# Layer statistics placed elsewhere on VectorE, norms turned into rows before they are stored, and the rounded transposed context written by a converting DMA

## The chip, the cores and the metric

One core of one Trainium2 chip runs the program. A core has five engines that run their own instruction lists and meet only at semaphores: TensorE (PE, matmuls; its weight loads are listed as PEld), VectorE (DVE), ScalarE (ACT), GpSimd (POOL) and SyncE (SP, here only a queue that issues DMAs). The metric is the time of one execution on the device in microseconds (us).

## The reference

```python
# x (16,128,1024), ctx (16,128,1024); q and k channels are the 128 rows, n = 1024 columns
qh = Wq @ layernorm(x);  kh = Wk @ ctx;  vh = Wv @ ctx        # 8 heads of 64
qh = softmax(qh, over the 64 of a head) * 64**-0.5
kh = softmax(kh, over n)
context = kh @ vh.T                                            # per head, 64 x 64
out = Wo @ (context.T @ qh) + bo
out = out / max(sqrt(sum(out*out, over channels)), 1e-12) * g * sqrt(128)
x = x + tanh(g_xattn) * out
# then a routed feed-forward part
y = layernorm(x);  scores = y @ Wr.T;  top 16 of 64, softmax -> G
x = x + tanh(g_ffn) * 2.0 * ((y @ A) * G) @ B                  # 64 experts of rank 16
```

## The kernel before

The 16 batches are tiles of 128 partitions x 1024 values (512 KB). The kernel has two stages: attention over all batches, then the feed-forward part over all batches. Every large product is done in three passes: each operand is split into a rounded half (`_hi`, type fp32r) and the remainder (`_lo = value - _hi`), and `three_pass` (L52 to L54) multiplies hi*hi, lo*hi and hi*lo into the same PSUM bank. ACT or a copy makes the `_hi` part, DVE or POOL the `_lo` part.

**The attention stage.** Each engine runs `body(b, head, tail, ahead)`: the head of batch b beside the tail of batch b-1, with a few steps for b+1 ahead. Bodies 0, 1, 15 and 16 are written out and bodies 2 to 14 are a loop. Nothing reorders instructions: each engine runs its list as the code has it, and a step that waits holds everything behind it on that engine. The steps that matter here, by the names in the code:

- DVE `stats(b+1)` (L720, L723), with the Newton steps for 1/sqrt(variance) in `inv_std` (L67, L58, L71, and three times L73, L75) and `nbias` (L728): the layer norm of the next batch. It stands after `lo_k(b, 0)` and before `sum_q(b, 0)` (L764, L767) and `lo_q(b-1, 2)` (L773, writes `qT_lo`).
- ACT `norm_x(b+1)` (L477) waits for `nbias`; ACT `hi_c(b)` (L498) rounds the transposed context `ctxT_in` into `ctxT_hi` (`cT[0]`).
- POOL, in order: `halve` of the last q pair (L370, `qhalf`), `lo_xn`, two `normalise` (L377, in place on `qe`), `halve(b,0)`, `mt_lo` (L417), `normalise(b,0)`, `lo_ctx(b+1)` twice (L349), `halve(b,1)`, `lo_c(b)` (L354, makes `ctxT_lo`), `normalise(b,1)`, `lo_xn(b+1,0)` (L361), `halve(b,2)`.
- PE `tr_k`, `tr_q` (L1075, L1084) transpose into one PSUM pair `psT`. Each waits until DVE has read what stood there before: `tr_k(b,1)` waits for `lo_q(b-1,2)`. Then `shift_q` (L1065) waits for `max_q` (L759), and `mm_k(b+1,0)` needs `ctx_lo` of the next batch.

**The norms.** `square_norms` (L1128) sums squares with matmuls against a column of ones, one column of 128 norms for each 128 columns of a batch, into `psX[:, 1, :]`; `keep_norms` (L734) copies them to `ss`, and `root_norms` (L745 to L749) makes `rn = 1/sqrt(ss)` on DVE, once for batches 0 to 12 (104 columns) at the start of body 15 and once for batches 13 to 15 (24 columns) after body 16. SP `store_norms` writes `rn` to DRAM (`rn_scratch`) as single words. `load_attention` then reads `u_scratch` (the unnormalised output) and a broadcast row of `rn_scratch`, after the wait for the store.

**Between the stages.** At the end of POOL's body 15 stands `residual(0,0,0)` (L389, L393): u times rn, plus x, for batch 0. Behind it on POOL stands `halve(15,3)`. DVE's body 16 runs `sum_q(15,2)`, `sum_q(15,3)`, `stats2(0,0)` (L812 to L819), then ACT `normalise(0,0)` (L577) and PE `tr_y(0,0)` (L1141) start the feed-forward stage; PE's `fold(15)` and `output(15)` stand behind `tr_y(0,0)`. PE's first `up` matmuls need `aT_lo` from `lo_weight` (L803). The second stage is a chain of matmuls with a period of about 25.5 us a batch.

## Time and profile before

| | us |
|---|---|
| median of 3 runs (1084.74 to 1086.72) | 1085.11 |
| the profiled execution, whole | 1085.12 |
| its span in the profile | 1083.1 |
| PE, DVE, ACT, POOL busy | 991.4, 701.7, 490.1, 470.8 |
| mean granted share of TensorE's clock | 0.976 |

The span runs from the first to the last recorded instruction. Busy time is not the bound by itself: an engine that waits in each body, and is waited for, sets the time. So the profile is read by the waits of PE and by the chain that ended last.

### The profile page before, as it was taken

Reading aid. Unit: us, or ns where it says so; the run is one execution under the profiler, and the core shown is the slowest. Engines: PE = TensorE matmul, PEld = TensorE weight load, DVE = VectorE, ACT = ScalarE, POOL = GpSimd, SP = SyncE. Lnnn points to the kernel's source line nnn. Section 1 sums busy time; section 2 is a strip of 40 time slices with the busy share of each in tenths; the row PEclk is TensorE's granted clock in tenths of the full one; section 3 lists DMA queues with packets and bytes.
Section 4 is the critical chain, followed back from the end, with each engine's and each line's share of the span. In section 5 each row is a group of like instructions: output and inputs, shape, how many; then the busy total and the mean of one; then the engine's idle time right before and its main releaser. Section 6 shows DMA issues by size and latency. Waiting matters only on the chain.

```text
span 1083.1 us, 15822 instructions
## 1 busy us (share of the span) xinstructions
PE 991.4 (92%) x5200; PEld 821.6 (76%) x5200; DVE 701.7 (65%) x1349; ACT 490.1 (45%) x791; POOL 470.8 (43%) x301
## 2 busy tenths in 40 slices
PE   4899999999999999999999673899999999999997
PEld 3677877787787778778778562788888888888886
DVE  5687677768777876876778368555555555555321
ACT  4675677567566756766675462121111221111110
POOL 2755665475556546555645464322222233333000
PEclk9999999999999999999999986899999999999999
DMA  3115121122012112201209942222222222222000
GB/s 136 59 58 205 59 77 36 42 77 70 27 58 77 39 39 77 77 20 58 77 19 21 156 168 66 78 87 104 82 78 77 78 77 77 77 77 77 20 19 39
DMA packets 38470, 77.15 MB, mean 71 GB/s; under 512 B 19376, under 2 KB 19376, under 8 KB 38448
## 3 DMA queue, kind: packets, MB, share of 16 engines
q1 hardware_dynamic: 37296, 75.83, 23.5%
q10 hardware_dynamic: 1152, 1.05, 0.3%
q8 instruction: 10, 0.16, 0.1%
q14 instruction: 12, 0.10, 0.0%
HBM read 60.03 MB, written 16.84 MB: 71 GB/s over the span
## 4 chain that ended last, share of the span: by engine, by line
PE 69%; DVE 19%; issue 5%; DMA 4%; ACT 1%; POOL 1%; DVEq 0%; SPq 0%; ACTq 0%; POOLq 0%
PE ps L52 18%; PE ps L54 18%; PE ps L53 18%; PE ps L1084 4%; DMA rn_scratch<-rn 3%; DVE qT_lo L773 3%; PE ps L1152 3%; PE ps L1075 3%; PE ps L1128 2%; PE ps L1065 2%; DVE ekT_lo L780 2%; DVE bn L720 2%; DVE qmax L759 2%; PE ps L1173 2%; DVE kmax L754 2%
## 5 line engine op out<-in xcount | busy, mean ns | idle before, releaser
L377 POOL TENSOR_TENSOR qe<-qe,qrec 128x1024 f32<-128x1024 f32 x64 | 121.2, 1903 | 134.5 <-DVE qrec L767 134.5
L400 POOL TENSOR_TENSOR yT_lo<-yf,yT_hi 128x512 fp32r<-128x512 f32 x32 | 41.8, 1327 | 269.0 <-ACT yT_hi L600 269.0
L370 POOL TENSOR_TENSOR qhalf<-qe 128x512 f32<-128x512 f32 x64 | 82.3, 1287 | 89.5 <-ACT qe L524 89.5
L52 PE MATMUL ps<-aT_hi,yT_hi 128*128 128x512 f32 x256 | 102.2, 399 | 5.9 <-DVE aT_lo L803 5.9
L773 DVE TENSOR_TENSOR qT_lo<-ps,qT_hi 128x512 fp32r<-128x512 f32 x128 | 81.5, 679 | 32.8 <-ACT qT_hi L531 32.3
L52 PE MATMUL ps<-bT_hi,hT_hi 128*128 128x512 f32 x256 | 101.6, 397 | 0.0
L54 PE MATMUL ps<-aT_lo,yT_hi 128*128 128x512 f32 x256 | 100.3, 392 | 0.0
L53 PE MATMUL ps<-aT_hi,yT_lo 128*128 128x512 f32 x256 | 100.3, 392 | 0.0
L588 ACT ACTIVATE yf<-ps 128x512 f32<-128x512 f32 x32 | 17.5, 594 | 183.0 <-PE ps L1141 182.9
L53 PE MATMUL ps<-bT_hi,hT_lo 128*128 128x512 f32 x256 | 100.1, 391 | 0.0
L54 PE MATMUL ps<-bT_lo,hT_hi 128*128 128x512 f32 x256 | 99.9, 390 | 0.0
L1075 PE MATMUL ps<-ident,ek 128*128 128x128 f32 x512 | 70.4, 278 | 30.2 <-DVE qT_lo L773 30.2
L1075 PEld LDWEIGHTS ps<-ident,ek 128*128 128x128 f32 x512 | 58.9, 141 | 45.4 <-DVE qT_lo L773 33.5
L524 ACT ACTIVATE qe<-ps 128x1024 f32<-128x1024 f32 x64 | 65.7, 1026 | 46.7 <-PE ps L1065 46.7
L780 DVE TENSOR_TENSOR ekT_lo<-ps,ekT_hi 128x512 fp32r<-128x512 f32 x128 | 81.9, 682 | 5.5 <-ACT ekT_hi L538 5.5
L759 DVE TENSOR_REDUCE qmax<-ps 128x16 fp32r<-128x1024 f32 x64 | 77.9, 1216 | 9.2 <-PE ps L54 9.2
L754 DVE TENSOR_REDUCE kmax<-ps 128x1 f32<-128x1024 f32 x64 | 78.0, 1218 | 5.2 <-PE ps L54 4.5
L538 ACT ACTIVATE ekT_hi<-ps 128x512 fp32r<-128x512 f32 x128 | 70.8, 601 | 22.9 <-PE ps L1075 22.8
L516 ACT ACTIVATE ek<-ps,kmax 128x1024 f32<-128x1024 f32 x64 | 71.8, 1122 | 15.6 <-DVE kmax L754 15.6
L604 ACT ACTIVATE hT_hi<-ps 128x512 fp32r<-128x512 f32 x32 | 19.1, 598 | 127.7 <-PE ps L1173 127.6
L531 ACT ACTIVATE qT_hi<-ps 128x512 fp32r<-128x512 f32 x128 | 70.7, 599 | 11.6 <-PE ps L1084 10.5
L872 DVE TENSOR_TENSOR hg<-ps,gate 128x512 f32<-128x512 f32 x32 | 22.1, 691 | 82.6 <-PE ps L54 82.5
(134 smaller groups left out, 2523.5 us busy)
## 6 DMA issues: line engine op xcount, KB each, us to landing
ctx_in<-in_ctx SPq DMA_DIRECT2D x16, 512.0 KB, 3.7
x_in<-in_x SPq DMA_DIRECT2D x16, 512.0 KB, 3.2
ctxT_in<-in_ctxT SPq DMA_DIRECT2D x16, 512.0 KB, 3.3
u_scratch<-osb SPq DMA_DIRECT2D x16, 512.0 KB, 2.8
x<-in_x SPq DMA_DIRECT2D x16, 512.0 KB, 4.0
u_in<-u_scratch SPq DMA_DIRECT2D x16, 512.0 KB, 3.4
rn_in<-rn_scratch SPq DMA_DIRECT2D x16, 512.0 KB, 4.3
out<-res SPq DMA_DIRECT2D x16, 512.0 KB, 2.9
```

Source lines behind the costliest of these rows:

```text
L52: nc.tensor.matmul(psum, whi, mhi, start=start, stop=False)
L53: nc.tensor.matmul(psum, wlo, mhi, start=False, stop=False)
L54: return nc.tensor.matmul(psum, whi, mlo, start=False, stop=stop)
L370: nc.gpsimd.tensor_tensor(qhalf[:, p % 2, :].rearrange("p (h d) -> p h d", d=DH // 2), v[:, :, 0:DH // 2], v[:, :, DH // 2:DH], ALU.add).t ...
L377: nc.gpsimd.tensor_tensor(v, v, w, ALU.mult).then_inc(q_norm, 1)
L516: nc.scalar.activation(ek[:, j % 2, :].rearrange("p (a n) -> p a n", a=HF), psK, ACT.Exp, bias=kmax[:, j:j + 1], accum_out=ksum[:, j:j + 1 ...
L538: nc.scalar.activation(ekT[0][:, 4 * h:4 * h + 4, j * P:j * P + P], psT[:, h, :].rearrange("p (n d) -> p n d", d=P), ACT.Copy).then_inc(k_ ...
L754: nc.vector.tensor_reduce(kmax[:, j:j + 1], psK, axis=AX.XY, op=ALU.max, negate=True).then_inc(k_max, 1)
L759: nc.vector.tensor_reduce(qmax[:, p % 2, :], psQ.rearrange("p a (h d) -> p (a h) d", d=DH), axis=AX.X, op=ALU.max, negate=True).then_inc(q ...
L773: nc.vector.tensor_tensor(qT[1][:, :, v], psT[:, h, :].rearrange("p (j n) -> p j n", n=P), qT[0][:, :, v].bitcast(f32), ALU.subtract).then ...
L780: nc.vector.tensor_tensor(ekT[1][:, n, w], psT[:, h, :].rearrange("p (n d) -> p n d", d=P), ekT[0][:, n, w].bitcast(f32), ALU.subtract).th ...
L1075: last = nc.tensor.transpose(psT[:, h, n * P:n * P + P], ek[:, j % 2, w:w + P], ident[:, :])
```

## The change

Four edits:

1. DVE: `stats(b+1)` (the two `bn_stats` and `bn_aggr`) moves between `sum_q(b-1,2)` and `sum_q(b-1,3)`; its Newton steps become `std(b+1, ...)`, five of them after `keep_norms(b-2)` and the last four with `nbias` after `max_k(b,1)`. `sum_q(b,0)` and `lo_q(b-1,2)` then follow `lo_k(b,0)` at once. This holds for bodies 1 to 14.
2. ACT's `hi_c(b)` is gone. POOL issues a DMA from DRAM into `ctxT_hi` after `normalise(b,0)`; `lo_c(b)` waits for it and for the plain load of `ctxT_in`, which stays.
3. The norms are turned: PE `tr_norms` transposes `rn` into `psX[:, 1, :]`, DVE `turn_norms` copies that to `rn_rows`, and SP stores rows of 128 words. In PE's body 15 this stands after `context(14,1)`, in the second case after the first `up` matmuls; on DVE it stands after `keep_norms(13)`, and after `route(0)`.
4. New waits: PE `fold(14)` waits for the first copy, `tr_h(0,0)` for the second.

```diff
             def store_norms(part, first, last):
-                sp.wait_ge(rn_step, NRT * (part + 1))
-                with nc.allow_non_contiguous_dma(reason="one norm to a word, in the order of the columns"):
-                    sp.dma_start(rn_dram[first:last].rearrange("o (k p) -> p (o k)", p=P),
-                                 rn[:, BK * first:BK * last]).then_inc(rn_stored, 16)
+                sp.wait_ge(rn_turned, part + 1)
+                sp.dma_start(rn_dram[first:last].rearrange("o (k p) -> (o k) p", p=P),
+                             rn_rows[0:BK * (last - first), :]).then_inc(rn_stored, 16)
...
+            def hi_c(b):
+
+                if started(b):
+                    pool.wait_ge(kc_mm, b)
+                nc.gpsimd.dma_start(cT[0][:, :, :].rearrange("p n c -> p (n c)"),
+                                    ctxT[bass.ds(b, 1)].rearrange("o p n -> (o p) n")).then_inc(c_hi, 16)
+
             def lo_c(b):
-                pool.wait_ge(c_hi, b + 1)
+                pool.wait_ge(ctxT_loaded, 16 * (b + 1))
+                pool.wait_ge(c_hi, 16 * (b + 1))
...
                 if head:
                     normalise(b, 0)
+                    hi_c(b)
...
-            def hi_c(b):
-                act.wait_ge(ctxT_loaded, 16 * (b + 1))
-                if started(b):
-                    act.wait_ge(kc_mm, b)
-                nc.scalar.activation(cT[0][:, :, :].rearrange("p n c -> p (n c)"), ctxT_in[:, :],
-                                     ACT.Copy).then_inc(c_hi, 1)
...
+            def turn_norms(part, rows):
+
+                dve.wait_ge(rn_T, part + 1)
+                if part > 0:
+                    dve.wait_ge(rn_stored, 16 * part)
+                nc.vector.tensor_copy(rn_rows[0:rows, :], psX[0:rows, 1, 0:P]).then_inc(rn_turned, 1)
...
+                if ahead and started(b):
+                    stats(b + 1)
+                if tail:
                     sum_q(b - 1, 3)
                 if head and started(b):
                     max_q(b, 0)
                 if late(b):
                     keep_norms(b - 2)
+                if head and not ahead:
+                    turn_norms(0, BK * FIRST)
+                if ahead and started(b):
+                    std(b + 1, range(5))
...
                 if head and started(b):
                     max_k(b, 1)
+                if ahead and started(b):
+                    std(b + 1, range(5, NCH + 1))
...
-                if ahead and started(b):
-                    stats(b + 1)
-                if head:
                     sum_q(b, 0)
...
             route(0)
+            turn_norms(1, BK * (NB - FIRST))
...
+                if isinstance(b, int) and b == NB - 2:
+                    pe.wait_ge(rn_turned, 1)
...
+            def tr_norms(part, first, last):
+                pe.wait_ge(rn_step, NRT * (part + 1))
+                pe.wait_ge(ss_read, NB - 2 if part == 0 else NB)
+                nc.tensor.transpose(psX[0:BK * (last - first), 1, 0:P], rn[:, BK * first:BK * last],
+                                    ident[:, :]).then_inc(rn_T, 1)
```

On DVE in the loop body, the piece from `lo_k(b,0)` on stands like this before (`ekT_lo` is `lo_k`, `qsum` and `qrec` are `sum_q`, `qT_lo` is `lo_q`):

```order
L780 TENSOR_TENSOR ekT_lo<-ps,ekT_hi 128x4x128
L718 ISA
L720 BN_STATS bn<-x_in 128x6 x2
L47 ISA
L723 BN_AGGR mv<-bn 128x2
L724 REGISTER_ALU
L67 TENSOR_SCALAR std_s<-mv 128x1
L63 ISA
L58 TENSOR_SCALAR rstd<-std_s 128x1
```

After the change the same place has no statistics, and the two q sums follow directly:

```order
L795 TENSOR_TENSOR ekT_lo<-ps,ekT_hi 128x4x128
L779 TENSOR_REDUCE qsum<-qhalf 128x16
L782 RECIPROCAL qrec<-qsum 128x16
```

The Newton steps stand after the change between `keep_norms` (`ss`), `lo_kc` (`kc_lo`), `max_k` (`kmax`) and `scale_m` (`mt`) of the same body:

```order
L742 TENSOR_SCALAR ss<-ps 128x8
L731 REGISTER_ALU
L67 TENSOR_SCALAR std_s<-mv 128x1
L63 ISA
L58 TENSOR_SCALAR rstd<-std_s 128x1
L71 TENSOR_SCALAR std_h<-mv 128x1
L65 REGISTER_ALU
L73 TENSOR_SCALAR std_t<-rstd,std_h 128x1
L65 REGISTER_ALU
L75 TENSOR_SCALAR rstd<-std_t,rstd 128x1
L800 TENSOR_TENSOR kc_lo<-ps,kc_hi 128x512
L768 REGISTER_ALU
```

So the statistics of b+1 are cut into three pieces that stand ahead of `sum_q(b-1,3)`, `lo_kc(b-1)` and `scale_m(b-1)`.

On POOL in the loop body before, `normalise(b,0)` (`qe`) is followed by the two `lo_ctx` (`ctx_lo`):

```order
L377 TENSOR_TENSOR qe<-qe,qrec 128x1024
L347 ISA
L349 TENSOR_TENSOR ctx_lo<-ctx_in,ctx_hi 128x512
L347 REGISTER_ALU
L349 TENSOR_TENSOR ctx_lo<-ctx_in,ctx_hi 128x512
```

After it, the DMA stands between them, and `ctxT_lo` four steps on waits for it:

```order
L386 TENSOR_TENSOR qe<-qe,qrec 128x1024
L357 ISA
L357 DMA ctxT_hi<-in_ctxT 128x1024
L349 ISA
L350 TENSOR_TENSOR ctx_lo<-ctx_in,ctx_hi 128x512
L348 REGISTER_ALU
L350 TENSOR_TENSOR ctx_lo<-ctx_in,ctx_hi 128x512
L375 REGISTER_ALU
L379 TENSOR_TENSOR qhalf<-qe 128x512
L361 REGISTER_ALU
L363 TENSOR_TENSOR ctxT_lo<-ctxT_in,ctxT_hi 128x1024
```

The issue of a DMA and the wait for its data have come into POOL's list, and one activation of 1024 columns has left ACT's.

## Rows read from the trace of the kernel before

**Rows 1.** Waits of PE, whole span: total us, times, longest us.
```profile
PE ps L1075 <- DVE qT_lo L773: 30.2, 16, 2.1
...
PE ps L1141 <- ACT u_in L577: 23.7, 2, 14.3
...
PE ps L1065 <- DVE qmax L759: 4.2, 14, 0.9
```

**Rows 2.** Busy us of each engine over one loop body, then clock and DMA.
```profile
339.20:376.90 37.70, 35.44 (x197) 29.05 (x197) 28.36 (x51) 24.73 (x41) 21.24 (x15) 1.00 0.16 55
```

**Rows 3.** Timeline, PE, one loop body: start, us, [idle before <- releaser].
```profile
367.84 1.25 PE L1075 MATMUL ps<-ident,ek 128*128 128x128 f32 x8 [1.98 <-DVE qT_lo L773]
...
370.69 0.70 PE L1065 MATMUL ps<-qmax,ident_r 128*128 128x512 f32 x2 [0.21 <-DVE qmax L759]
```

**Rows 4.** Timeline, DVE, the same body.
```profile
347.89 0.69 DVE L764 TENSOR_REDUCE qsum<-qhalf 128x16 f32<-128x512 f32 x1 [2.44 <-POOL qhalf L370]
...
352.75 0.69 DVE L785 TENSOR_TENSOR kc_lo<-ps,kc_hi 128x512 fp32r<-128x512 f32 x1 [2.05 <-ACT kc_hi L544]
...
356.22 1.41 DVE L797 TENSOR_TENSOR mt<-ps,krec 64x512 f32<-64x512 f32 x2 [1.51 <-PE ps L54]
...
362.32 1.28 DVE L720 BATCH_NORM_STATS2 bn<-x_in 128x6 f32<-128x512 f32 x2
...
366.27 0.68 DVE L764 TENSOR_REDUCE qsum<-qhalf 128x16 f32<-128x512 f32 x1
...
367.15 1.22 DVE L773 TENSOR_TENSOR qT_lo<-ps,qT_hi 128x512 fp32r<-128x512 f32 x2
```

**Rows 5.** Timeline, ACT, the same body.
```profile
363.26 1.08 ACT L531 ACTIVATE qT_hi<-ps 128x512 fp32r<-128x512 f32 x2
...
366.39 1.24 ACT L477 ACTIVATE xn<-x_in,nbias,rstd 128x1024 f32<-128x1024 f32 x1 [2.05 <-DVE nbias L728]
```

**Rows 6.** Timeline, POOL, the same body.
```profile
367.31 1.90 POOL L377 TENSOR_TENSOR qe<-qe,qrec 128x1024 f32<-128x1024 f32 x1 [7.66 <-DVE qrec L767]
...
369.17 2.53 POOL L349 TENSOR_TENSOR ctx_lo<-ctx_in,ctx_hi 128x512 fp32r<-128x512 f32 x2
...
372.89 2.41 POOL L354 TENSOR_TENSOR ctxT_lo<-ctxT_in,ctxT_hi 128x1024 fp32r<-128x1024 f32 x1
```

**Rows 7.** DMA issues: KB each, median us from issue to landing.
```profile
ctxT_in<-in_ctxT SPq DMA_DIRECT2D x16, 512.0 KB, 3.3
...
b_raw<-in_BT SPq DMA_DIRECT2D x8, 512.0 KB, 7.9
...
rn_scratch<-rn SPq DMA_DIRECT2D x1, 52.0 KB, 31.9
```

**Rows 8.** Timeline, the DMA queue of SP: start and length of an issue.
```profile
375.45 0.33 SPq L241 DMA_DIRECT2D ctxT_in<-in_ctxT  x1
```

**Rows 9.** Timeline, DVE, `root_norms` at the start of body 15.
```profile
573.35 0.27 DVE L745 TENSOR_TENSOR rn_t<-rn,ss 128x104 f32<-128x104 f32 x1
...
574.25 1.28 DVE L745 TENSOR_TENSOR rn_t<-rn,ss 128x104 f32<-128x104 f32 x1
```

**Rows 10.** Timeline, POOL, bodies 15 and 16.
```profile
574.11 1.29 POOL L370 TENSOR_TENSOR qhalf<-qe 128x512 f32<-128x512 f32 x1 [3.51 <-ACT qe L524]
...
601.90 1.29 POOL L370 TENSOR_TENSOR qhalf<-qe 128x512 f32<-128x512 f32 x1
...
616.28 2.34 POOL L389 TENSOR_TENSOR rn_in<-u_in,rn_in 128x1024 f32<-128x1024 f32 x1 [13.10 <-DMA rn_in<-rn_scratch]
...
621.06 1.25 POOL L370 TENSOR_TENSOR qhalf<-qe 128x512 f32<-128x512 f32 x1
```

**Rows 11.** Timeline, ACT and PE, bodies 15 and 16.
```profile
607.91 1.03 ACT L524 ACTIVATE qe<-ps 128x1024 f32<-128x1024 f32 x1 [1.63 <-PE ps L1065]
...
628.58 1.97 PE L1141 MATMUL ps<-ident,u_in 128*128 128x128 f32 x8 [14.33 <-ACT u_in L577]
```

**Rows 12.** Busy us of PE (instructions), granted clock, DMA, after that wait.
```profile
628.50:633.20 4.70, 4.62 (x24) 0.56 0.00 0
```

More of the change, by code:

```diff
@@ L112, in flamingo_layer @@
         rn_t = small("rn_t", [P, NB * BK])
+        rn_rows = small("rn_rows", [P, P])
         bn2 = small("bn2", [P, 2, 6])
@@ L187, in flamingo_layer @@
         m_mm, m_scaled, m_hi, m_lo = sem("m_mm"), sem("m_scaled"), sem("m_hi"), sem("m_lo")
-        o_mm, o_sq, o_out, ss_mm, ss_read, rn_step = (
-            sem("o_mm"), sem("o_sq"), sem("o_out"), sem("ss_mm"), sem("ss_read"), sem("rn_step"))
+        o_mm, o_sq, o_out, ss_mm, ss_read, rn_step, rn_T, rn_turned = (
+            sem("o_mm"), sem("o_sq"), sem("o_out"), sem("ss_mm"), sem("ss_read"), sem("rn_step"),
+            sem("rn_T"), sem("rn_turned"))
         u_stored, rn_stored = sem("u_stored"), sem("rn_stored")
@@ L654, in body @@
                     exp_k(b, 3)
-                    hi_c(b)
                 if tail:
@@ L723, in stats, with std @@
                 nc.vector.bn_aggr(mv[:, :], bn[:, :, :].rearrange("p a b -> p (a b)")).then_inc(stats_step, 1)
-                dve.wait_ge(stats_step, NS * b + HF + 1)
-                for k in range(NCH):
-                    inv_std(dve, k, mv[:, 1:2], rstd[:, :], std_s[:, :], std_h[:, :], std_t[:, :], std_step, NCH * b)
-                dve.wait_ge(std_step, NCH * (b + 1))
-                nc.vector.tensor_scalar(nbias[:, :], mv[:, 0:1], -1.0, rstd[:, :], ALU.mult,
-                                        ALU.mult).then_inc(nbias_done, 1)
+            def std(b, steps):
+                for k in steps:
+                    if k == 0:
+                        dve.wait_ge(stats_step, NS * b + HF + 1)
+                    if k < NCH:
+                        inv_std(dve, k, mv[:, 1:2], rstd[:, :], std_s[:, :], std_h[:, :], std_t[:, :], std_step, NCH * b)
+                    else:
+                        dve.wait_ge(std_step, NCH * (b + 1))
+                        nc.vector.tensor_scalar(nbias[:, :], mv[:, 0:1], -1.0, rstd[:, :], ALU.mult,
+                                                ALU.mult).then_inc(nbias_done, 1)
             def keep_norms(b):
@@ L895, in _ @@
             stats(0)
+            std(0, range(NCH + 1))
             for n, w in enumerate((wk, wq)):
@@ L920, in body @@
                     max_k(b, 1)
+                if ahead and started(b):
+                    std(b + 1, range(5, NCH + 1))
                 if not started(b):
                     stats(b + 1)
+                    std(b + 1, range(NCH + 1))
                 if tail and not head:
@@ L1170, in tr_h @@
                     pe.wait_ge(h_lo, 2 * b + g)
+                else:
+                    pe.wait_ge(rn_turned, 2)
                 for n in range(4):
@@ L1206, in body @@
                     context(b - 1, 1)
+                if head and not ahead:
+                    tr_norms(0, 0, FIRST)
                 if head:
@@ L1268, in _ @@
                     square_norms(NB - 1)
+            tr_norms(1, FIRST, NB)
             def ffn_body(b, half, nxt):
```

## The prediction

> **What bounds the kernel now.** I began with the chain that ended last. In the attention stage it goes round through PE, DVE and ACT in every body; in the feed-forward stage it is PE alone. So I read next what PE waits for over the whole span [rows 1]. Three entries carry nearly all that the change can touch: `tr_k` waits for DVE's `qT_lo` 16 times, 30.2 us together, the transposes of `u_in` wait 23.7 us in two waits, the longer of 14.3, and `shift_q` waits for `qmax` 14 times, 4.2 us. The third view is the busy time over one loop body [rows 2]. The stretch is one body; its steps come back every 37.67 us. PE is busy for 35.44 of them, at the full granted clock, DVE 28.36, ACT 24.73, POOL 21.24. PE is therefore the bound but for a little over 2 us a body, and the reader is to see in the timeline where these lie: 1.98 us before `tr_k(b,1)` and 0.21 before `shift_q(b,2)` [rows 3]. Before the first, DVE works off the statistics of the next batch, which start at 362.32 and hold `sum_q` back to 366.27 and `qT_lo` to 367.15 [rows 4], while ACT had begun the matching `qT_hi` at 363.26 [rows 5]. DVE itself idles elsewhere in the same body: 2.44, 2.05 and 1.51 us before `qsum`, `kc_lo` and `mt` [rows 4].
>
> At the seam of the stages there is one long wait. The store of 104 columns of norms as single words takes 31.9 us [rows 7]; `residual(0,0,0)` on POOL sits idle for 13.10 us until its data is there, at 616.28, and the `halve` behind it starts at 621.06 [rows 10]. PE resumes at 628.58 after 14.33 idle [rows 11].
>
> **The statistics, bodies 1 to 14.** What is moved takes from 362.32 to about 366.3 on DVE, 4 us. The first piece (two `bn_stats`, 1.28, and `bn_aggr`, about 0.4 with its wait) goes into the 2.44 us before `sum_q(b-1,3)`: 0.8 to spare. The five first Newton steps, about 1 us, go into the 2.05 before `kc_lo`: 1 to spare. The last four and `nbias`, from 365.0 to 366.35 or 1.35 us, go into the 1.51 before `mt`: 0.15 to spare. So these gaps cover all of it; were one filled too early or too late, its excess would reach PE through `kc_lo` or `mt`, at most the 0.5 us or so by which the pieces could stretch.
> At the old place `sum_q(b,0)` now starts at 362.4 and ends, with its reciprocal, at 363.3. `qT_lo` then waits for ACT: the first half of `qT_hi` is done at 363.8, the second at 364.35 [rows 5], so the halves of `qT_lo` (1.22 for both [rows 4]) end at about 364.5 and 365.1. PE gets to `tr_k(b,1)` at 367.84 - 1.98 = 365.86 [rows 3]: no wait, 0.8 to spare. `max_k(b,3)` and `max_q(b,2)`, 1.13 each in the pipeline of DVE, end at 367.4; PE wants the second at 365.86 + 0.87 + 1.37 = 368.1. No wait. What is late next is `ctx_lo` or the exponential before `mm_k(b+1,0)`: `nbias` is ready at 356, so ACT's `xn` starts at 364.35 in place of 366.39 [rows 5] and everything behind it is also 2 us earlier, as PE is. That keeps the old distances there. I take the whole 1.98 + 0.21 = 2.19 us, 14 times: **-30.7 us**. From below: PE busy 35.44 in 37.67 leaves 2.23 a body, so not over -31.2. From above: if other waits give half of it back, -15.
>
> **The converting DMA.** ACT loses one activation of about 1.05 us a body, and is not the bound; I count nothing. POOL gains the issue, behind `normalise(b,0)` and ahead of `ctx_lo`. The trace has no DMA issued by POOL. The nearest rows are 0.33 us, an issue on SP's queue [rows 8], and 2.41 us, POOL's own pass over the same tile [rows 6]. I take 1 us, nearer to the first, since an issue touches no 1024 columns. `normalise(b,0)` waited 7.66 us for `qrec` [rows 6], and `qrec` is now ready 4 us earlier: it runs from 363.3 to 365.2, the issue to 366.2, the two `ctx_lo` (2.53 [rows 6]) to 368.7. PE wants the second half of `ctx_lo` at about 370.9 (before 2.19 earlier, 373.1, behind the transposes that start at 371.3). So the issue is hidden up to 1 + 2.2 = 3.2 us, and above that each us costs a us a body. The landing: plain loads of the same tile take 3.3 us, one of eight loads together 7.9 [rows 7]. I take 4, so the data is there at 370.2, when POOL has also done `halve(b,1)`. Behind the wait stand `ctxT_lo` 2.41, `normalise` 1.9, `xn_lo` 1.25 and `halve(b,2)` 1.25, in all 6.8 us, and DVE wants the last at 380.0; so the data may land as late as 373.2, or 7 us after the issue, for nothing.
> POOL and DVE do get in each other's way in this trace: `rn_t` takes 0.27 us and, started while POOL is in an operation of 1.29 us, 1.28 [rows 9, 10]. The DVE operations beside the new issue are `qT_lo` and `kmax`, which read PSUM and show no such stretching beside POOL.
> The Trainium skill (SBUF — State Buffer, the box on the "DVE blocks DMA" trap) says that a DMA issued by GpSimd has its descriptors written by GpSimd, and that a VectorE operation in a two-port mode locks it out meanwhile. By it the DMA would begin up to one such operation later; this case's trace agrees on the exclusion as far as the 1.28 against 0.27 goes, and has no such DMA. It would eat 1 of the 3 us to spare at the landing and leave the sum as it is.
>
> **The norms.** SP's store of 104 rows of 512 bytes replaces 13312 words. Its bounds are the 31.9 us of before and the 3.3 us of a 512 KB load [rows 7]; I take 3. It can be out by 584, and the load of `u_in` and `rn_in` behind it by 592. POOL reaches `residual(0,0,0)` when `halve(15,2)` ends, at 601.90 + 1.29 = 603.2 [rows 10]: so not the DMA but POOL's own list decides. Its two operations take 2.34 each and 0.14 between, to 608.1. `halve(15,3)` needs `qe`, ready at 607.91 + 1.03 = 608.94 [rows 11]. So it starts at 608.94 in place of 621.06: **-12.1 us**, and the chain from it to PE's `u_in` transposes stays 628.58 - 621.06 = 7.5 us long. PE arrives at 614.1 and waits 2.4 in place of 14.33.
> After the long wait PE ran 4.7 us at a granted 0.56 [rows 12], its lower level of 1.2 GHz. With 2.4 us idle it may stay at 2.4 GHz, as in most loop bodies after their 1.98. The transposes would take 0.9 less and the fold 1.1 less, partly behind `kc_lo`: **-1.5 us**, bounds 0 and -2.
> Added: the transposes and copies. In body 15 `tr_norms` waits for `keep_norms(13)`, late by the 5 us of `root_norms`, and holds `mm_k(15,1)`: 0.1 to 1 us, I take 0.5. `turn_norms(1)` waits on DVE until the first `up` is through, with `bT_lo` and `stats2(1,1)` behind it: I take +0.5, bounds 0 and 1. The feed-forward loop is untouched.
>
> **Sum.** Against the profiled execution of 1085.12 (span 1083.1 and 2.0 around it, which agrees with the median of 1085.11): -30.7 - 12.1 - 1.5 + 0.5 + 0.5 = -43.3, or 1041.8. Two bodies of the loop ran part of their time at the lower clock after that wait of 1.98, which might go too; I round down to **1041.5 us**.
>
> **Rivals.**
> *A. The issue holds POOL for longer than 3.2 us.* For it: nothing in the trace shows an issue by POOL, and POOL's operations are long. Against: 0.33 on SP. An issue of 4.5 us costs 1.3 x 14 = 18: about 1060.
> *B. Other waits take the place of the 1.98.* For it: ACT's chain `qT_hi`, `xn`, `ctx_hi`, `ekT_hi`, exponential up to `mm_k(b+1,0)` has only some 0.5 us to spare, `mt` 0.15. Half of the loop's gain goes: 1057.
> *C. Slower: POOL is held in every body by issue or landing.* If the data lands later than 7 us after the issue, `halve(b,2)`, `qsum`, then the statistics behind it and `qmax` come late, and PE stands at `shift_q(b,0)`. Each us beyond costs 14. It makes the kernel slower than before from 7 + 43.3 / 14 = 10.1 us on; at 11 us the time is 1041.5 + 4 x 14 = 1097. For it: the word-wise store shows how badly many small pieces go. Against: 512 KB in rows of 4 KB lands in 3.3, and in 7.9 at worst.
> *D. The store stays slow,* and PE's wait at the seam with it; only the loop gains: 1085.1 - 30.7 = 1055. Against: it now has whole rows of 512 bytes; and anything under 20 us is hidden.
>
> **How the numbers follow.** The forecast has 0.66, its own range 1036 to 1047. A has 0.12, B 0.13, C 0.04, D 0.03, and 0.02 is for a loop that gains more than PE's gaps show. The range for 8 in 10: the lower end is 31.2 + 12.1 + 2 with no additions and a little for the clock, 1037 and a margin, so 1035; the upper takes in B and half of A: 1058. A difference under 0.2%, 2 us, is what a measurement of this kernel can't tell from none. Faster: all but C and the far tail of A, 0.95; same 0.01; slower 0.04.
>
> **What would show it.** In the changed profile: a body of 35.5 us; the wait of `tr_k` for `qT_lo` gone from PE's list; idle of DVE before `qsum`, `kc_lo` and `mt` under 1 us each; POOL's `ctx_lo` starting within 1.5 us of the end of `qe`, and `ctxT_lo` without a long wait for the DMA; the norm store landing in some 3 us, `halve(15,3)` right behind ACT's `qe`, PE's wait for `u_in` some 2.4 us. Wrong would be: PE waiting for `ctx_lo` or `ek` before `mm_k`, POOL idle 3 us and more before `ctxT_lo`, or a body over 36.5 us.

## The result and the profile after

The changed kernel takes 1029.85 us, median of 4 runs (1028.69 to 1033.63), against 1085.59 for the kernel before beside it (4 runs). The ratio is 0.949, interval 0.947 to 0.952: faster by 55.7 us, where 43.6 was forecast. The direction was right, and the time lies 5 us below the range. The profiled execution has a span of 1028.3, 54.8 less than before, and I account for that difference.

I set the two traces side by side at the same steps of the work: the start of ACT's `kc_hi` in body 1 and in body 15 (`kc_hi(1)` and `kc_hi(15)` from here on), which enclose 14 bodies, then PE's transposes of `u_in`, the point where PE starts again after its wait for `aT_lo` (behind the second norms on DVE), and the second transposes of `u_in`.

| stretch | before | after | difference | forecast |
|---|---|---|---|---|
| start to `kc_hi(1)` | 49.96 | 51.52 | +1.6 | 0 |
| 14 loop bodies | 529.91 | 484.68 | -45.2 | -30.7 |
| to PE's `u_in` transposes | 48.71 | 36.99 | -11.7 | -12.1, and +0.5 for `tr_norms` |
| to PE's start behind the stretch of the second norms | 31.39 | 31.58 | +0.2 | -1.5 (clock) |
| to the second `u_in` transposes | 14.00 | 14.38 | +0.4 | +0.5 |
| from there to the end | 409.13 | 409.15 | 0.0 | 0 |

Most of what was out lies in the loop; the start (+1.6) and the clock gain that did not come (1.7) went the other way. Eleven of the fourteen bodies took about 37.67 us before, three 38.4 to 38.6. Each of these three has one stretch of 3.4 us at a granted clock of 0.50 (from 66.0, 520.0 and 557.6 us); the changed kernel has none in its fourteen. Now every body takes 34.62: 14 x 3.05 = 42.7, and 2.5 from those three. One body of after, by engine (start and end, length, busy us of PE, PE's weight loads, DVE, ACT and POOL with their instructions, clock, DMA share and GB/s), answers to [rows 2]:

```profile
321.00:355.60 34.60, 34.54 (x198) 29.31 (x198) 28.13 (x51) 23.46 (x39) 21.78 (x15) 1.00 0.22 75
```

PE is busy for all but 0.06 us. But it was busy for 35.44 in the body of before, and the work is the same. So 0.9 of those 35.44 were not work; what they were is the question of the next lines. The list of PE's waits over the whole span answers to [rows 1]:

```profile
PE ps L1173 <- ACT u_in L580: 11.9, 2, 9.6
...
PE ps L52 <- DVE aT_lo L818: 6.0, 1, 6.0
...
PE ps L1099 <- DVE qT_lo L788: 2.1, 2, 1.1
PE ps L1089 <- DVE qmax L774: 1.8, 3, 0.9
```

The 30.2 us behind `qT_lo` have become 2.1, the 23.7 behind `u_in` 11.9, and there is no new wait in the loop. These entries explain 14 x 2.2 us of the loop. Where is the rest? PE's timeline shows it if one reads from start to start, not the idle time alone. Before, around the wait of [rows 3]:

```profile
365.47 0.39 PE L54 MATMUL ps<-wq_lo,xn_hi 128*128 128x512 f32 x1
...
368.84 0.48 PE L52 MATMUL ps<-qT_hi,mt_hi 128*128 128x512 f32 x1
...
371.29 1.25 PE L1084 MATMUL ps<-ident,qe 128*128 128x128 f32 x8
```

After, at the same steps:

```profile
341.90 0.39 PE L54 MATMUL ps<-wq_lo,xn_hi 128*128 128x512 f32 x1
342.14 1.03 PE L1099 MATMUL ps<-ident,ek 128*128 128x128 f32 x8
342.93 0.48 PE L52 MATMUL ps<-qT_hi,mt_hi 128*128 128x512 f32 x1
...
344.39 0.60 PE L1089 MATMUL ps<-qmax,ident_r 128*128 128x512 f32 x2
344.83 0.60 PE L1108 MATMUL ps<-ident,qe 128*128 128x128 f32 x4
```

A matmul of 512 columns is recorded as 0.39 us, and the next one starts 0.23 us behind it. The record of the last one before a stall covers 0.16 us of the stall. From the last `mm_q` matmul to `tr_k(b,1)` it was 2.37 us and is 0.24: 2.13 gained, of which the wait list showed 1.98. `tr_k(b,1)` itself went from 1.00 (367.84 to 368.84) to 0.79, the output half behind it (368.84 to 370.69) from 1.85 to 1.46, with only 0.21 listed, and `shift_q` from 0.60 to 0.44. The transposes `tr_q(b-1,3)` went from 1.01 to 0.79. Together 2.13 + 0.21 + 0.39 + 0.16 + 0.22 = 3.1 us, the 3.05 of the body. That much is a sum of distances; that it comes from the order on DVE, and how much of it, is tested below.

On DVE the three pieces are in the gaps where they were meant to be ([rows 4] had 2.44, 2.05 and 1.51 there):

```profile
324.30 0.69 DVE L779 TENSOR_REDUCE qsum<-qhalf 128x16 f32<-128x512 f32 x1 [0.91 <-POOL qhalf L379]
...
329.19 0.69 DVE L800 TENSOR_TENSOR kc_lo<-ps,kc_hi 128x512 fp32r<-128x512 f32 x1 [1.19 <-ACT kc_hi L547]
...
332.66 1.41 DVE L812 TENSOR_TENSOR mt<-ps,krec 64x512 f32<-64x512 f32 x2 [0.27 <-PE ps L54]
...
340.32 1.29 DVE L788 TENSOR_TENSOR qT_lo<-ps,qT_hi 128x512 fp32r<-128x512 f32 x2 [0.60 <-ACT qT_hi L534]
```

Each gap is shorter and none is gone, and `qT_lo` now waits for ACT. On POOL the new issue stands between `qe` and `ctx_lo` ([rows 6]):

```profile
339.80 1.91 POOL L386 TENSOR_TENSOR qe<-qe,qrec 128x1024 f32<-128x1024 f32 x1 [3.71 <-DVE qrec L782]
341.65 0.59 POOL L357 DMA_DIRECT2D ctxT_hi<-in_ctxT  x1
342.51 2.53 POOL L350 TENSOR_TENSOR ctx_lo<-ctx_in,ctx_hi 128x512 fp32r<-128x512 f32 x2 [0.27 <-ACT ctx_hi L495]
...
346.25 2.38 POOL L363 TENSOR_TENSOR ctxT_lo<-ctxT_in,ctxT_hi 128x1024 fp32r<-128x1024 f32 x1
```

The issue holds POOL for 0.59 us, and `ctxT_lo` does not wait for the data, which lands in 3.7 us (the median of 16):

```profile
ctxT_hi<-in_ctxT POOLq DMA_DIRECT2D x16, 512.0 KB, 3.7
```

At the seam, SP issues the norms at 537.08 and already at 538.69 the load of `u_in`, which stands behind the end of that store: it took at most 1.6 us instead of 31.9 [rows 7] (the trace has no landing for this store).

```profile
537.08 0.41 SPq L251 DMA_DIRECT2D rn_scratch<-rn_rows  x1
...
538.69 0.34 SPq L243 DMA_DIRECT2D u_in<-u_scratch  x1
```

POOL no longer waits 13.10 us for `rn_in` [rows 10]; PE waits 2.34 in place of 14.33 [rows 11], and 0.41 more for `kc_lo`:

```profile
559.72 2.39 POOL L398 TENSOR_TENSOR rn_in<-u_in,rn_in 128x1024 f32<-128x1024 f32 x1
...
565.62 1.30 POOL L379 TENSOR_TENSOR qhalf<-qe 128x512 f32<-128x512 f32 x1 [1.01 <-ACT qe L527]
```

```profile
573.19 1.09 PE L1173 MATMUL ps<-ident,u_in 128*128 128x128 f32 x8 [2.34 <-ACT u_in L580]
574.69 0.58 PE L52 MATMUL ps<-wvo_hi,kc_hi 128*128 128x256 f32 x1 [0.41 <-DVE kc_lo L800]
575.07 0.41 PE L53 MATMUL ps<-wvo_hi,kc_lo 128*128 128x256 f32 x1
575.28 0.41 PE L54 MATMUL ps<-wvo_lo,kc_hi 128*128 128x256 f32 x1
```

### The profile page after: what moved, and what is told of

The parts are those of the page before. It is cut to its first block, busy times and chain, and to the rows that moved or that the text cites. A ratio compares the mean times of both kernels' runs of the same rounds, so it can differ in the third digit from the quotient of the medians.

```text
span 1028.3 us, 15861 instructions
## 1 busy us (share of the span) xinstructions
PE 978.9 (95%) x5202; PEld 822.7 (80%) x5202; DVE 699.2 (68%) x1351; ACT 471.1 (46%) x775; POOL 480.4 (47%) x317
## 4 chain that ended last, share of the span: by engine, by line
PE 83%; DVE 10%; issue 5%; ACT 1%; DMA 1%; POOL 0%; DVEq 0%; SPq 0%; ACTq 0%
PE ps L52 21%; PE ps L54 21%; PE ps L53 21%; PE ps L1108 6%; PE ps L1099 4%; PE ps L1184 3%; PE ps L1154 3%; DVE qT_lo L788 2%; PE ps L1089 2%; PE ps L1207 2%; DVE mt L812 1%; DVE ekT_lo L795 1%; PE ps L1173 1%; DVE qmax L774 1%; DVE rn_t L753 1%
## 5 line engine op out<-in xcount | busy, mean ns | idle before, releaser
L534 ACT ACTIVATE qT_hi<-ps 128x512 fp32r<-128x512 f32 x128 | 69.5, 598 | 13.3 <-PE ps L1108 12.4
L1108 PE MATMUL ps<-ident,qe 128*128 128x128 f32 x512 | 69.6, 276 | 2.5 <-DVE qT_lo L788 1.4
L1108 PEld LDWEIGHTS ps<-ident,qe 128*128 128x128 f32 x512 | 58.2, 140 | 16.8 <-DVE ekT_lo L795 8.3
```

The lines of the kernel that those rows point to most:

```text
L1108: last = nc.tensor.transpose(psT[:, h, j * P:j * P + P], qe[:, p, w:w + P], ident[:, :])
```

## The experiments

Times are medians. The kernel before was run again in each of the three series (1085.13 us for `e1` to `e4`, 1089.11 for `e5` to `e8`, 1087.67 for `e9` to `e12`), and ratios are against it; the changed kernel was run only beside the first result, where the kernel before took 1085.59. So a difference between the changed kernel and a run of a later series carries 2 to 4 us of the series, and the smaller ones are read from the traces; "body" is the period of a loop body, "seam" the time from `kc_hi(15)` to the first rounding of `u_in` on ACT, 47.41 us before and 35.70 after. Where one run is named, its time is that of one execution.

### Each part alone

`e1_stats_only`: the kernel before with edit 1 alone.

```diff
+                if ahead and started(b):
+                    stats(b + 1)
                 if tail:
                     sum_q(b - 1, 3)
...
+                if ahead and started(b):
+                    std(b + 1, range(5))
...
+                if ahead and started(b):
+                    std(b + 1, range(5, NCH + 1))
...
-                if ahead and started(b):
-                    stats(b + 1)
                 if head:
                     sum_q(b, 0)
```

> The kernel before with only the statistics moved. Theory H (hidden stalls): the body shrinks by more than the 2.19 us that PE's list of waits shows, because each wait of PE also holds short stalls that are booked as busy; all of the 3.07 us of a body that the changed kernel saved comes from removing the late qT_lo. But with ScalarE still rounding the context (1.05 us in front of qT_hi of pair 3) I expect some 0.3 to 0.6 us of a body back as a wait of tr_k(b,2): body 34.9 to 35.2 us, time 1085.6 - 14 x 2.6 = about 1048 (1043 to 1052); the seam keeps its 14 us wait. Rival S (my prediction's sum): the body takes 35.5 us or more and the time is 1055, the rest having come from the lighter ScalarE. Rival N: the move alone gives nothing without the DMA, 1080 and more.

Measured: 1045.46 us (1043.83 to 1045.84), ratio 0.961 to 0.965. Body 34.94, seam 46.86. A change that touches only DVE's order takes 2.73 us out of a body whose listed waits were 2.19 (theory H; 34.9 to 35.2 was expected for the body), and PE's busy time over the kernel falls from 991.4 to 983.7 us with the same 5200 instructions:

```profile
PE 983.7 (94%) x5200; PEld 822.1 (79%) x5200; DVE 699.9 (67%) x1349; ACT 485.4 (47%) x791; POOL 472.3 (45%) x301
```

So stalls were inside "busy", and 0.54 of the 0.86 us a body that the forecast missed belong to the statistics.

`e2_dma_only`: the kernel before with edit 2 alone.

```diff
-                nc.scalar.activation(cT[0][:, :, :]..., ctxT_in[:, :], ACT.Copy).then_inc(c_hi, 1)
+                nc.gpsimd.dma_start(cT[0][:, :, :]..., ctxT[bass.ds(b, 1)]...).then_inc(c_hi, 16)
```

> The kernel before with only the rounded context written by GpSimd's converting DMA. Theory H: nothing in the loop, since PE waits for the qT_lo that stands behind the statistics on VectorE; body 37.67, time within 2 us of 1085.6, with the 1.6 us later start-up of the changed kernel if that comes from this DMA. Rival S: ScalarE's relief is worth 0.88 us a body by itself: 1073.

Measured: 1088.45 us (1084.02 to 1090.45, 10 runs), ratio 1.002 to 1.004: slower by 3.3, where at most 2 was expected. Body 37.67, as before. The trace has a wait that neither kernel has, before `context(15)`, and it comes from POOL:

```profile
612.21 0.76 PE L52 MATMUL ps<-ekT_hi,ctxT_hi 128*128 128x512 f32 x1 [4.59 <-issue]
```

```profile
593.01 0.59 POOL L358 DMA_DIRECT2D ctxT_hi<-in_ctxT  x1
...
609.76 2.34 POOL L364 TENSOR_TENSOR ctxT_lo<-ctxT_in,ctxT_hi 128x1024 fp32r<-128x1024 f32 x1 [14.86 <-DMA ctxT_hi<-in_ctxT]
```

The DMA of body 15, issued at 593.01, lands only at 609.6, after 16.6 us. The 13312 words of the norms are being stored on SP's queue meanwhile, from 577.22 to 610.73, and the DMA lands 1.1 us before that store although it stands on another queue. In the changed kernel the same DMA, issued beside the same `root_norms` but with no such store under way, lands in 3.7. "Issue" as the releaser of a PE wait here means that the profile did not name it; POOL's row does.

This wait does not explain the 3.3 us. The profiled execution is the fastest of the ten, 1084.02, with the wait in it: the next wait, for `u_in`, is 8.98 instead of 14.33, so that the seam is only 0.7 longer (48.13 against 47.41). The start is 0.8 later, the stretch from the `u_in` transposes to the second ones 2.2 shorter and the rest 0.7 longer. What makes the median 3.3 longer stays open.

`e3_norms_only`: the kernel before with edits 3 and 4 alone.

```diff
-                    sp.dma_start(rn_dram[first:last].rearrange("o (k p) -> p (o k)", p=P), rn[...])
+                sp.dma_start(rn_dram[first:last].rearrange("o (k p) -> (o k) p", p=P), rn_rows[...])
```

> The kernel before with only the norms stored as rows. Both theories: loop unchanged, the seam 11.7 us shorter: 1085.6 - 11.5 = 1074 (1073 to 1075). If the seam in the changed kernel were shorter because of the DMA or the new order, this would give less.

Measured: 1073.47 us (1072.37 to 1076.52), ratio 0.987 to 0.993: -11.7. Body 37.67, seam 36.06, so 11.35 come from the seam, as worked out in the forecast to 0.3 us.

`e4_no_dma`: the changed kernel with the rounding back on ACT (edit 2 undone).

```diff
-                nc.gpsimd.dma_start(cT[0][:, :, :]..., ctxT[bass.ds(b, 1)]...).then_inc(c_hi, 16)
+                nc.scalar.activation(cT[0][:, :, :]..., ctxT_in[:, :], ACT.Copy).then_inc(c_hi, 1)
```

> The changed kernel with the rounding of the context back on ScalarE (statistics moved, norms as rows). Theory H: the changed kernel plus the 0.3 to 0.6 us a body by which qT_hi of pair 3 comes late: 1034 to 1038. Rival S: the DMA is worth 0.88 us a body, 1042. If the start-up of the changed kernel is 1.6 us later because of the DMA, its first kc_hi is back at 50.0 us here.

Measured: 1032.51 us (1031.58 to 1033.66), 2.7 slower than the changed kernel and just below the span expected. Body 34.97, 0.35 longer; that is 4.9 us over the loop. It is spread over PE's matmuls `mm_k(b+1,0)` (1.72 us from start to start, 1.48 with the DMA) and `tr_k(b,2)` (0.91 and 0.79), again with no entry in PE's waits. Of the 4.9 the start gives back 1.5, and the stretch between the two transposes of `u_in` 3.05. The latter is no virtue of the edit: 1.2 of it is the clock, which stayed at its upper level in the fold here (below), and the rest is left of 4.2 that `root_norms(1)` gains on DVE because it happened to meet less of POOL's work, and 2.1 that `gate` loses because it met more.

With these four the difference is taken apart: statistics -39.7, norms -11.7, the DMA +3.3 alone and -2.7 with the two others. The sum of the single parts is -48.1 and the whole is -55.7. Most of the missing 7.6 is the DMA in the loop: it gives nothing while `qT_lo` stands behind the statistics, and 4.9 us once they are moved. The store in rows may add something, if it takes away what held up the DMA.

`e9_no_norms` tests both: the changed kernel with the word-wise store put back and edits 3 and 4 out, which is also the statistics and the DMA together.

```diff
-                sp.dma_start(rn_dram[first:last].rearrange("o (k p) -> (o k) p", p=P), rn_rows[...])
+                    sp.dma_start(rn_dram[first:last].rearrange("o (k p) -> p (o k)", p=P), rn[...])
```

> The changed kernel with the norms stored as single words again. Theory Q: the 13312 words do not only delay u_in; GpSimd's own DMA of body 15, issued while they drain, lands late too, so ctxT_lo and PE's context(15) wait, as one run with the DMA alone showed (4.6 us before context(15)). Then the seam is longer than the 11.7 us that the store cost in the kernel before: 1029.9 + 11.7 + 2 to 5 = 1044 to 1047. Rival: the two do not meet, 1041.5.

Measured: 1043.69 us (1040.74 to 1044.62), 44.0 under the kernel before of its series. The two parts alone add up to -36.4, so the 7.6 stand between the statistics and the DMA; the body is 34.63 with the DMA and 34.94 in `e1_stats_only` without it. The norms are worth 11.8 on top when each kernel is set against its own kernel before, and 13.8 when the two times are compared directly; alone they had been worth 11.7. The times therefore do not show that the two meet. The trace does. The same wait is there, longer, since the loop ends earlier against the same store:

```profile
571.26 0.77 PE L52 MATMUL ps<-ekT_hi,ctxT_hi 128*128 128x512 f32 x1 [7.63 <-issue]
```

```profile
568.82 2.34 POOL L364 TENSOR_TENSOR ctxT_lo<-ctxT_in,ctxT_hi 128x1024 fp32r<-128x1024 f32 x1 [17.88 <-DMA ctxT_hi<-in_ctxT]
```

The DMA, issued at 549.03, lands at 568.69, the word-wise store at 569.71. The seam is 50.6 us here and 46.86 in `e1_stats_only`, which differs by the DMA alone: the hold-up costs 3.7 us there, and the shorter loop gives 4.3 back. That the transfer is held up by the store is shown by these landings; its price by the seams of one execution each. The time came out just below the span I had given for it, in part because the wait before `context(15)` shortens the next one for `u_in` (8.05 instead of 13.78).

### How much room the loop has

DVE gets 2, 4 or 6 reductions of 0.6 us each just before `sum_q(b,0)`, over a weight tile, with a result that nobody reads.

```diff
                     lo_k(b, 0)
+                if ahead and started(b):
+                    for k in range(2):    # 4, 6
+                        nc.vector.tensor_reduce(pad[:, k:k + 1], wq[0][:, :].bitcast(f32), axis=AX.X, op=ALU.max)
+                if head:
                     sum_q(b, 0)
```

> The changed kernel with 2 reductions over a constant tile (512 columns, some 0.6 us each) on VectorE where the statistics stood, in the 14 bodies that have them. Theory H: the loop is held by several places behind qT_lo, each with its own small slack (qmax, ekT_lo), of which the smallest counts: 0.9 us of room, then one for one. With 1.3 us the body grows by about 0.4, to 35.0. Rival W (only the wait that the list names): 1.7 us of room before tr_k(b,1) waits, so no growth, 34.6.

> The same with 4 reductions, some 2.5 us. Theory H: body 34.62 + 2.5 - 0.9 = 36.2, while PE's list shows a wait of about 0.7 to 1.0 us a body: the rest is in gaps booked as busy, so PE's busy time rises with no instruction added. Rival W: 35.4.

> The same with 6 reductions, some 3.8 us, about the length of the statistics. Theory H: body 37.5, PE's busy time back near 990 us, listed waits for qT_lo near 2.0 us a body. Rival W: 36.7 and busy unchanged at 979.

Measured, one execution each: 1033.87, 1051.39 and 1065.23 us, with bodies of 34.94, 36.11 and 37.32. So 1.2 us of delay cost 0.32, 2.4 cost 1.49 and 3.64 cost 2.70. Beyond the first 0.9 us each us costs one us. The forecast had given `tr_k(b,1)` a room of 0.8. The steps show once more what the wait list leaves out: PE's busy time is 978.9 us in the changed kernel and 981.9, 990.6 and 987.8 in these three, with the same 5202 instructions. In `e7_pad6` PE's list says

```profile
PE ps L1104 <- DVE qT_lo L789: 24.1, 16, 1.6
```

about 1.6 us a body, with 0.2 more for `qmax`, where the body grew by 2.70; with 1.2 us of delay the body grew by 0.32 and the list shows no wait in the loop at all.

### What is left at the seam

`e8_stats2_first`: the changed kernel, with the statistics of the first feed-forward batch ahead of the last `sum_q` on DVE.

```diff
-                if tail:
+                if tail and head:
                     sum_q(b - 1, 3)
...
                     stats2(0, 0)
+                    sum_q(b - 1, 3)
                     lo_weight(0)
```

> The changed kernel with VectorE's stats2(0,0) ahead of sum_q(15,3) in body 16. Theory: what is late at the seam now is stats2 behind sum_q(15,3), which waits 2.27 us for qhalf; x of batch 0 is ready at 564.6, PE arrives at 570.9. So u_in comes 2.3 to 3 us earlier and PE waits under 0.3 us there; its clock should then stay at the upper level in the fold behind (which took the lower one after 2.34 + 0.41 us idle), 0.5 to 1.5 us more. In all 2.3 to 4 us: 1026 to 1027.5. Rival: the seam is held by PE's own list or by the fold's kc_lo behind aT_lo on VectorE, and the gain is under 1 us.

Measured: 1025.03 us (1024.63 to 1025.97), 4.8 less than the changed kernel (4.3 between the traces), where at most 4 was expected. The seam is 32.49, PE waits for `u_in(0)` no more, and the fold runs at the full granted clock:

```profile
571.23 0.28 PE L54 MATMUL ps<-wvo_lo,kc_hi 128*128 128x256 f32 x1
571.34 0.28 PE L52 MATMUL ps<-wvo_hi,kc_hi 128*128 128x256 f32 x1
```

Here the matmuls of 256 columns follow each other in 0.12 us; in the changed kernel, behind 2.34 us and 0.41 us of idle, in 0.21 (575.07 to 575.28 above). These windows give the clock, of the changed kernel

```profile
572.50:576.50 4.00, 2.90 (x16) 2.67 (x17) 3.33 (x4) 3.06 (x6) 0.45 (x1) 0.72 0.96 372
576.00:582.00 6.00, 4.56 (x28) 3.87 (x28) 3.44 (x6) 3.00 (x6) 1.27 (x1) 0.86 0.13 55
```

and of `e8_stats2_first`

```profile
570.00:577.00 7.00, 5.52 (x43) 4.80 (x42) 5.42 (x10) 5.08 (x11) 5.41 (x3) 1.00 0.83 300
```

Mean values of 0.72 and 0.86 are a mixture of the two levels, 1.2 and 2.4 GHz: in the changed kernel the clock stands at 0.50 from 574.3 to 577.7. From the `u_in` transposes to the `qe` transposes behind the fold it takes 2.29 us in `e8_stats2_first` and 4.22 in the changed kernel, as in the kernel before. But the wait need not be gone for that: in `e4_no_dma` and `e7_pad6`, with the same waits of 2.36 or 2.32 and then 0.4 us, the clock is 1.00 throughout (575 to 582 and 609 to 616 us) and the stretch takes 3.0. In the six other kernels with a wait of 2.3 us there it fell. What decides between the two is open.

`e10_weights_first`: the changed kernel, with `lo_weight(6)` and `lo_weight(7)` ahead of `keep_norms` and `root_norms(1)` on DVE, since PE waits 6.03 us for `aT_lo` behind them.

```profile
604.77 0.80 PE L52 MATMUL ps<-aT_hi,yT_hi 128*128 128x512 f32 x1 [6.03 <-DVE aT_lo L818]
```

```diff
+            lo_weight(6)
+            lo_weight(7)
             keep_norms(NB - 1)
             root_norms(1, FIRST, NB)
-            lo_weight(6)
-            lo_weight(7)
```

> The changed kernel with aT_lo of parts 6 and 7 ahead of keep_norms(15) and root_norms(1) on VectorE, in its 5.1 us of idle before them. Theory L: the second half of the seam is set by root_norms(1), 10.2 us because four of its ten small operations stand behind GpSimd's operations, and the weights behind it. Its place ahead of route and stats2(1,1) stays, so only the 2.3 us of aT_lo leave the path to u_in: PE's wait for aT_lo (6.0 us) is gone, its wait for u_in grows by some 3.7, and the time falls by 2 to 2.5 us, to 1027.5. Rival P: PE's matmuls are the bound there and all 6 us are won: 1024.

Measured: 1029.17 us (1027.74 to 1030.56), a gain of 0.7 us (1.4 between the traces), where 2 to 2.5 was expected, and the runs do not tell it from none. The wait moved on: PE now waits for `rn` and longer for `u_in(1)`.

```profile
PE ps L1173 <- ACT u_in L580: 15.2, 2, 12.8
...
PE ps L1161 <- DVE rn L757: 3.9, 1, 3.9
```

Why `root_norms(1)` is that slow is to be read on DVE in the changed kernel, with 24 columns in each of these operations:

```profile
593.37 1.88 DVE L58 TENSOR_SCALAR rn<-ss 128x24 int32<-128x24 int32 x1
595.28 2.32 DVE L753 TENSOR_TENSOR rn_t<-rn,ss 128x24 f32<-128x24 f32 x1
597.64 0.18 DVE L755 SCALAR_TENSOR_TENSOR rn_t<-rn_t,rn 128x24 f32<-128x24 f32 x1
...
598.73 2.37 DVE L753 TENSOR_TENSOR rn_t<-rn,ss 128x24 f32<-128x24 f32 x1
601.13 0.18 DVE L755 SCALAR_TENSOR_TENSOR rn_t<-rn_t,rn 128x24 f32<-128x24 f32 x1
601.35 2.23 DVE L757 SCALAR_TENSOR_TENSOR rn<-rn_t,rn 128x24 f32<-128x24 f32 x1
```

and on POOL at the same time:

```profile
592.82 2.40 POOL L402 TENSOR_TENSOR x<-rn_in,x 128x1024 f32<-128x1024 f32 x1
595.17 2.39 POOL L390 TENSOR_TENSOR bT_lo<-b_raw,bT_hi 128x1024 fp32r<-128x1024 f32 x1
598.72 2.34 POOL L398 TENSOR_TENSOR rn_in<-u_in,rn_in 128x1024 f32<-128x1024 f32 x1 [1.16 <-DMA rn_in<-rn_scratch]
601.21 2.34 POOL L402 TENSOR_TENSOR x<-rn_in,x 128x1024 f32<-128x1024 f32 x1
```

Four operations end within 0.04 us of the end of one of POOL's (593.37 + 1.88 = 595.25 against 595.22, and so on); those that start while POOL idles take 0.18. In `e4_no_dma` only two of them were caught: from the first of these operations to `aT_lo` it takes 5.92 us there and 10.14 here.

`e11_late_root`: the weights stand as in `e10_weights_first` and `keep_norms(15)` stays, but the roots, the transpose and the copy of the last norms go behind the first half batch of the feed-forward stage, and `stats2(1,1)` behind `route(0)`.

```diff
-            root_norms(1, FIRST, NB)
             dve.wait_ge(gf_done, 1)
             route(0)
-            turn_norms(1, BK * (NB - FIRST))
...
                 if nxt:
                     route(b + 1)
+                if not started(b):
+                    root_norms(1, FIRST, NB)
                 result(b, slot, 2 * i + slot // 2)
+                if not started(b):
+                    turn_norms(1, BK * (NB - FIRST))
...
             ffn_body(0, 0, True)
+            tr_norms(1, FIRST, NB)
```

> As e10, and root_norms(1), tr_norms(1), turn_norms(1) after the first down projection instead of ahead of route(0); stats2(1,1) directly behind route(0). Theory L: u_in of batch 1 then starts some 12 us earlier (VectorE: 3.3 us for the route and 3.9 for the statistics after 593.2, so PE's transposes near 602 to 606 instead of 619), and about 10 to 13 us are won: 1017 to 1020. The stored norms are late by some 30 us but needed two batches on. Rival: the bT weights or their loads bind next and under 6 us are won, 1024 or more.

Measured: 1026.55 us (1025.08 to 1027.31), 3.3 less than the changed kernel. From the first to the second rounding of `u_in` on ACT it takes 33.61 us in place of 45.96, the 12.4 that were expected. But 9 of them were given back later, and the reason is a thing I had overlooked: SP waits for the store of these norms before it loads the attention result of batch 3 as well. The norms are on their way at 633.10, and POOL gets its data at 641:

```profile
641.12 2.39 POOL L402 TENSOR_TENSOR rn_in<-u_in,rn_in 128x1024 f32<-128x1024 f32 x1 [17.59 <-DMA rn_in<-rn_scratch]
```

On DVE `stats2` of that batch then waits for POOL, and in the order of DVE's list stands ahead of the gating that PE needs now:

```profile
646.05 1.29 DVE L831 BATCH_NORM_STATS2 bn<-x 128x6 f32<-128x512 f32 x2 [5.51 <-POOL x L406]
...
650.00 0.68 DVE L891 TENSOR_TENSOR hg<-ps,gate 128x512 f32<-128x512 f32 x1
```

```profile
650.74 1.11 PE L1207 MATMUL ps<-ident,hg 128*128 128x128 f32 x4 [4.35 <-DVE hg L891]
```

Aligned at the second transposes of `u_in`, the rest of the kernel takes 9.8 us longer than in the changed kernel. At the first transposes of `hg` it is 1.8 behind (PE waits 5.92 there instead of 4.12), at the `hg` of 650.74 it is 6.9. Behind that stall the granted clock is 0.51 from 649.9 to 656.8, the products of 512 columns follow each other in 0.43 us instead of 0.23, and 2.9 more are lost; then the distance stays at 9.8.

`e12_best`: the edits of `e8_stats2_first` and `e11_late_root` together.

> e11 and e8 together. If the two halves of the seam are independent the gains add: 1029.9 - 4.8 - 11 = about 1014 (1012 to 1017). If e8's gain is eaten by the second half: 1018 and more.

Measured: 1021.97 us (1021.21 to 1023.82, 5 runs), ratio 0.938 to 0.941, the fastest of all. The gains of the two add up (4.8 + 3.3 = 8.1, measured 7.9; all three compare across series). I had expected 1014, because the 9 us that `e11_late_root` gives back were not known yet.

## Why the prediction was right and where it failed

*What bounds the kernel.* Right: PE, and its waits for `qT_lo` and `u_in`. But "PE is busy for 35.44 of them" was read as work.

*The statistics.* The mechanism is as described: the late `qT_lo` held PE, and moving the statistics alone frees it (`e1_stats_only`). The pieces fit into their gaps with 0.91, 1.19 and 0.27 us left, `qT_lo` waits for ACT, and the room of 0.8 us at `tr_k(b,1)` measured 0.9. The step that failed is the size: "I take the whole 1.98 + 0.21 = 2.19 us" and, with it, "PE busy 35.44 in 37.67 leaves 2.23 a body, so not over -31.2". Measured are 3.05 us a body, 2.73 by the statistics alone (`e1_stats_only`) and 0.3 by the DMA beside them. Idle time in the list starts only where a matmul's record ends, and part of the time lost around a stall is booked as busy; 0.5 us a body lay there for the statistics, 7.6 over the loop. The other 0.3, 4.5 over the loop, belong to the DMA, which the forecast had put at nothing. The bound was none. Allowing for it with 0.02 ("a loop that gains more than PE's gaps show") was far too little; this, too, is why the range was missed. The terms named for the lower end, 31.2 + 12.1 + 2, give 1039.8; the 2.8 us from there to 1037, "a little for the clock", no row had priced.

*The slower bodies.* The forecast named two and rounded 0.3 us for them. They were three, each with a stretch at the lower clock, and gave 2.5 us.

*The converting DMA.* "I count nothing": alone this is right for the loop's body (37.67 in both), and the kernel is 3.3 slower for a reason that the trace does not show; with the other parts it is -2.7 in all and -4.9 in the loop. This is the second step that failed: with PE's long stall gone, "ACT loses one activation ... and is not the bound" no longer means nothing. The terms were near: the issue 0.59 us against 1 taken, the landing 3.7 against 4. By the rule of the Trainium skill (SBUF — State Buffer, the box on the "DVE blocks DMA" trap) the landing could have been later by an operation of DVE. The converting DMA lands in 3.7 us and the plain load of the same tile in 3.2; a hold-up of over 0.5 us does not show in this median.

*The norms.* Right: -12.1 with +0.5 for `tr_norms`, measured -11.7. `tr_norms` starts 0.66 us behind the last matmul of `context(14,1)` (536.43 against 535.77) where 0.23 is the usual distance, and the next product's second matmul follows 0.6 us later than usual, so it costs about 0.5. PE's wait for `u_in` is 2.34, forecast 2.4. The store takes 1.6 us at most, not 3. The forecast did not see that the word-wise store would hold up the new DMA, which the rows avoid.

*The clock.* Wrong: -1.5 was counted, nothing came. The transposes are 0.9 shorter as counted (1.09 for 1.97), but 0.41 went to the wait for `kc_lo`, and the clock fell at 574.3, so that the fold ran at the lower level. `e4_no_dma` has the same waits, kept the clock and gained 1.2 us: the gain was there, and that the changed kernel missed it is, as far as these traces tell, chance.

*The second half.* `turn_norms(1)` +0.5, measured +0.4. The start of the kernel, taken as unchanged, is 1.6 us later. To `kc_hi(1)` it is 50.0 to 50.1 us in three kernels without the DMA, 50.8 in `e2_dma_only`, which differs from the kernel before by the DMA alone, and 50.8 to 51.2 in eight others with it: some 0.8 to 1.2 us are the DMA's. The changed kernel (51.5) and `e1_stats_only` (50.9, without the DMA) have a stretch at the lower clock on the way, from 34.9 and 34.1 us on, and that is the rest.

*The rivals.* A is excluded by the 0.59 us, C by the POOL rows without a wait before `ctxT_lo` in the loop (in body 15, where no `ctx_lo` stands between, it waits 1.96 us, and PE does not wait for it), D by SP's rows. B (other waits take half) did not occur: none is on PE's list in the loop. That a body is 0.35 us shorter with the DMA than without speaks for ACT's chain up to `mm_k(b+1,0)` being as near as B said, and for the DMA having shortened it. The 0.35 is shown by two pairs of kernels; that ACT's chain is the reason is argued from the distances in `e4_no_dma`, not shown.

In all, the forecast's -43.3 and the traces' -54.8 differ by the statistics (-7.6), the DMA in the loop (-4.5), the slower bodies (-2.5), the start (+1.6) and the clock (+1.7), to within 0.2 us.

## What to carry to other kernels

To size what the end of a stall gives, compare the starts of the same steps in a body with a wait and in one without, or at least the distance between neighbouring matmuls; neither PE's busy share nor the sum of its listed waits is a bound. When a period is bound by PE, a piece of work on another engine that is moved ahead of a wait costs nothing until its room is used up, and from there one for one. Store small results in rows, and look at what else moves through the DMA engines meanwhile: a store of single words delayed a transfer on another queue by 13 to 16 us. Set a kernel against one run in the same series, or compare traces step by step: here the kernel before itself moved by 4 us from series to series, as much as some of the gains. Before norms, or any result, are made later, list all that wait for their store, also by the order of an engine's list.

## What the runs showed of the hardware

- PE's busy time includes stalls: 991.4 us before, 983.7 with the same 5200 instructions in another order on DVE; 978.9 after, 990.6 with the same 5202 and 2.4 us of delay on DVE in each body. A record of 0.39 us at a distance of 0.23 hides 0.16 at each stall.
- A DMA from GpSimd that converts 512 KB from f32 to the rounded type holds POOL for 0.59 us and lands in 3.7.
- A store of 13312 single words delayed such a DMA on another queue: it landed in 16.6 us in `e2_dma_only` and 19.7 in `e9_no_norms`, about 1 us before the store itself, against 3.7 without it.
- DVE's operations of 24 columns from SBUF to SBUF take 0.18 us, and 1.88 to 2.37 when they meet an operation of POOL; they then end with it. Those of one column were not held: `nbias` takes 0.21 us in all 16 batches of the changed kernel, 14 times beside an operation of POOL.
- Around a wait of PE of 2.3 us and one of 0.4 behind it the granted clock fell to 0.50 in six kernels and stayed at 1.00 in two (`e4_no_dma`, `e7_pad6`); each of the three slower bodies before has 3.4 us at 0.50.
